# Message phase of a four-layer graph network on one core: TensorE takes the message products first in each turn

## What is computed

```python
et = edge_emb_W[edge_type]
m = relu(concat([x[src], et]) @ msg_W.T + msg_b)
agg = segment_sum(m, dst) / clip(deg, 1)
h = x + agg @ upd_W.T + upd_b
x1 = (h - mean(h)) * rsqrt(var(h) + 1e-5) * ln_g + ln_b
x  = layernorm(x + x1)
```

## Time and profile before

| | before |
|---|---|
| median of 3 runs | 2558.56 us (2558.45 to 2558.84) |
| profiled execution, its own time | 2568.89 us |
| its span | 2567.1 us |
| busy: TensorE | 1396.4 us (54%) |
| busy: VectorE | 1565.7 us (61%) |
| busy: ScalarE | 861.6 us (34%) |
| busy: GpSimd | 1825.5 us (71%) |
| mean granted clock of TensorE | 0.761 |

### The profile page before, as it was taken

One profiled execution on the slowest core, in us unless ns is written; L12 is line 12 of the kernel. 1 busy time (PEld: TensorE's weight loads), 2 busy tenths in 40 slices (PEclk: granted clock), 3 DMA queues, 4 the chain that ended last, 5 costly groups with the idle time before them and its releaser, 6 DMA issues. The chain is left out here.

```text
span 2567.1 us, 21864 instructions
## 1 busy us (share of the span) xinstructions
PE 1396.4 (54%) x4580; PEld 726.2 (28%) x4580; DVE 1565.7 (61%) x4901; ACT 861.6 (34%) x1813; POOL 1825.5 (71%) x1444
## 2 busy tenths in 40 slices
PE   6788488887455456619698376445454650011111
PEld 1344244444222222303343144222222330011110
DVE  8889377778537776967989544233344555434433
ACT  0111166776425455754687322011012320000000
POOL 5764677787188888617666388788775878778887
PEclk8899699999677777859899688677777875555555
DMA  1111244443244554625565476577796873323331
GB/s 24 26 34 37 78 114 134 123 125 91 75 101 98 127 127 111 149 63 126 123 148 141 84 215 194 135 200 173 173 170 195 224 200 93 85 63 72 75 71 43
DMA packets 358129, 297.95 MB, mean 116 GB/s; under 512 B 110941, under 2 KB 312428, under 8 KB 357981
## 3 DMA queue, kind: packets, MB, share of 16 engines
q1 hardware_dynamic: 260397, 225.43, 32.5%
q0 software_dynamic: 97600, 71.11, 14.5%
HBM read 199.75 MB, written 96.70 MB: 115 GB/s over the span
## 5 line engine op out<-in xcount | busy, mean ns | idle before, releaser
L2201 DVE TENSOR_TENSOR_SCAN tl_S<-tl_same,tl_S,tl_pX 128x500 f32<-128x500 bf16 x96 | 120.3, 1253 | 324.4 <-issue 172.6
L2090 PE MATMUL tl_pX<-k_ident,tl_ga 125*128 125x125 f32 x400 | 84.1, 348 | 428.3 <-DMA tl_ga<-table_TE,k_s_idxE 328.2
L480 POOL DMA_INDIRECT tl_ga<-table_TE,k_s_idxE x200 | 244.2, 1221 | 63.4 <-issue 58.8
L2090 PEld LDWEIGHTS tl_pX<-k_ident,tl_ga 125*128 125x128 f32 x400 | 57.5, 177 | 443.8 <-DMA tl_ga<-table_TE,k_s_idxE 338.7
L480 POOL DMA_INDIRECT eq_ga<-table_T,k_idxS x100 | 128.0, 1280 | 65.5 <-ACT eq_y L1794 37.3
L480 POOL DMA_INDIRECT at_ga<-x,k_src x100 | 139.5, 1395 | 43.4 <-issue 25.2
L480 POOL DMA_INDIRECT ms_ga<-table_T,k_idxS x100 | 143.3, 1433 | 36.4 <-issue 30.2
L480 POOL DMA_INDIRECT tl_ga<-table_TH,k_send x100 | 122.6, 1226 | 56.3 <-issue 55.7
L1270 PE MATMUL tl_pCon<-dr_BC,dn_cT 128*128 128x512 f32 x196 | 130.5, 754 | 54.0 <-ACT dn_cT L1277 27.3
L282 POOL DMA_INDIRECT table_ptab<-k_ef,ix_scatI x100 | 124.2, 1242 | 48.8 <-issue 48.8
L480 POOL DMA_INDIRECT at_gb<-xw,at_dstI x100 | 129.8, 1298 | 30.5 <-issue 30.5
(11 more groups left out here) (465 smaller groups left out, 4406.2 us busy)
## 6 DMA issues: line engine op xcount, KB each, us to landing
dr_x<-x SPq DMA_DIRECT2D x97, 256.0 KB
result<-dr_o SPq DMA_DIRECT2D x97, 256.0 KB
dm_xT<-xT SPq DMA_DIRECT2D x32, 768.0 KB
tl_fac<-table_dinv SPq DMA_DIRECT2D x50, 250.0 KB
table_T<-at_y SPq DMA_DIRECT2D x50, 224.0 KB
table_T<-ms_y SPq DMA_DIRECT2D x50, 224.0 KB
table_T<-eq_y SPq DMA_DIRECT2D x50, 224.0 KB
table_TE<-tl_y SPq DMA_DIRECT2D x50, 224.0 KB
```

The costliest lines, as they stand in the source:

```text
L480: nc.gpsimd.indirect_dma_start(out=buf[:, k, :], out_offset=None, in_=table, in_offset=bass.IndirectOffsetOnAxis(ap=index[:, CT * c + k:CT ...
L2090: last = nc.tensor.transpose(pX[j % 2][:, k * TP:(k + 1) * TP], ga[j % RG][:, k, :], K["ident"][0:TP, 0:TP])
L2201: nc.vector.tensor_tensor_scan(S[i][:], same[j % RM][:], pX[i][:, 0:CE], 0.0 if j % NC == 0 else S[1 - i][:, CE - 1:CE], ALU.mult, ALU.add ...
```

## The change

In TensorE's loop of the message phase, the step `message(s + 1)` moves from behind `turn(s + 2)` to the head of the turn. The order becomes message products, row transposes, transposes of gathered rows, update, moments. The steps themselves, their waits and their semaphores, and all other engines, stay as they are.

```diff
             for s in range(-2, NC + 1):
+                if live(s + 1):
+                    message(s + 1)
                 if live(s - 1):
                     rows(s - 1)
                 if live(s + 2):
                     turn(s + 2)
-                if live(s + 1):
-                    message(s + 1)
                 if live(s):
                     update(s)
                     dn.moments(pe, MA + s)
```

## The result

| | before | after |
|---|---|---|
| median of the runs (11 each) | 2558.84 us | 2565.99 us |
| ratio, 95% interval | | 1.0026 [1.0015, 1.0038] |
| profiled span | 2567.1 us | 2565.5 us |
| busy: TensorE | 1396.4 us | 1421.5 us |
| busy: VectorE | 1565.7 us | 1581.2 us |

The kernel became slower by 0.26%, 6.7 us by the ratio (7.2 by the medians); 5.4 us were forecast. The span of the profiled execution is 1.6 us shorter than before's, against the median. What follows therefore reads stretches, and says under e7 and e8 where the 1.6 us come from. VectorE's 15.5 us more of busy time are not the order's: a second profile of after (e8) has 1567.4 us.

What follows compares the result with a forecast made beforehand. GpSimd's DMA issues, then VectorE's queue after about 1003 us, were taken to bound the message phase. 0.54 + 0.70 + 2.1 + 2.1 = 5.4 us on 2558.56 gave 2564.0 us, range 2558.2 to 2568.5 us.

Steps and rivals of the forecast that it cites:

- What bounds the phase: Message phase: GpSimd's DMA issues set the pace to about 1003 us, then VectorE's queue, ten turns in 120.4 us.
- rival C: GpSimd's gathers: fewer long instructions, gather 9 us earlier, 2555 us, chance 0.08; mirror, +9 us and more, 0.06.
- the last gather-bound transposes: Sign in TensorE's turn 16: again near 1003 us; over 2 us off 1003.17 would mean GpSimd's pace depends on the order.
- Earlier message products gain nothing: ScalarE's relu of the message products stays behind its own `source` and `norm1`; value 0.
- The products' own time: Turns after s = 16 and 20: 1.68 us of products delay transposes; less slack, 0.54 + 0.70 us late.
- The clock under moments: TensorE at s = 16 and 20: `moments` starts at half clock after an idle gap, +2.1 us each.
- Rival A: TensorE's clock rises despite the gap in one or both turns: +3.3 or +1.24 us, 2559.8 to 2561.9 us; chance 0.22.
- Where the wait shows: VectorE's `gained` after turns 16 and 20 would wait about 2.6 and 2.8 us for `norm1`, where before had none.
- Rival B: Late transposes in turn 17 stay hidden by VectorE's slack: 2558.6 us, at most half a us from before; chance 0.12.
- From the profile to the medians: Whole kernel: profiled execution 2568.89 to 2574.3 us; its 10.3 us above the median carried over, giving 2564.0 us.
- the question of 0.2%: Whole kernel against the 5.1 us bound: slower by over 0.2% chance 0.45, within 0.49, faster 0.06.

Runs made afterwards that it cites:

- e7: The unchanged kernel before, profiled once more for scatter; 121.8 us from `gained(14)` to `gained(24)`, against 120.4 us in its first profile.
- e8: The changed kernel after, profiled once more for scatter; 126.3 us from `gained(14)` to `gained(24)`, as in its first profile.
- e4: Against after: eight products of the identity, never read, added behind `update` in turns with s % 4 = 0; median 2566.62 us, ratio 0.9999 to before.
- e2: Against after: message products back behind the transposes of gathered rows in turns with s % 4 = 0 only; median 2570.34 us, ratio 1.0012 to before.
- e1: Against after: VectorE's `keep_moments` moved ahead of `residual`, so `moments` needn't wait for it; median 2568.49 us, ratio 1.0011 to before.
- e9: Against before: VectorE's `keep_moments` moved ahead of `residual`, TensorE's order as in before; ratio 0.9996 to before, 119.7 us from `gained(14)` to `gained(24)`.

## Why the prediction held

*What bounds the phase.* Right. The end of the phase is the last gather awaited plus VectorE's queue. The part of GpSimd scatters by several us and took no side; rival C, faster or slower through GpSimd, has nothing for it. One of the prediction's own signs did show against it: the last gather-bound transposes came at 1000.67, more than 2 us off 1003.17. The sign was too tight, for in e7 the unchanged kernel came 2.4 us off.

*Earlier message products gain nothing.* Right: in after ScalarE's relu of turn 16 starts right behind its `norm1` as before, and no step of VectorE from `gained(14)` on became shorter.

*The products' own time, 0.54 + 0.70 us.* Right in mechanism and size: with the clock up, e4 shows 0.57 and 0.85, e2 0.57 in the one turn with a fast start.

*The clock under moments, 2.1 us twice.* Right in mechanism; the first was 1.97 us, the second 2.7. In the three profiles of after the first lies between 1.5 and 2.0 us and the second between 2.5 and 2.7, so 2.1 was near the first and too small for the second. That the step had to be priced from one stretch of another burst, and came out this near, is partly luck. In turn 20 the way there differs too: the clock was up over the transposes and fell in a wait for `ms_mean` that the products used to fill. The sum with the measured values is 1.68 + 1.97 - 1.14 = 2.5 and 1.68 + 2.7 - 0.98 = 3.4 us; the steps grew by 2.54 and 3.36. What failed is the silent assumption that before always has the clock up at this point. In e7 it had not, in both turns; so the difference of the two orders is 4.5 to 6 us, not one number. Rival A, that the clock is up when `moments` starts in after, came in none of the 15 late `moments` of its three profiled executions.

*Where the wait shows.* Partly wrong. I expected 2.6 and 2.8 us ahead of `gained`. VectorE reaches `residual` first, which waits for the row transposes, so 1.29 and 2.14 us appear there and only 1.09 and 1.08 us ahead of `gained`. The sum is 5.6 us, against 5.4.

*Rival B (hidden anyway)* holds only where `moments` isn't late: e1 and e9.

*From the profile to the medians.* The forecast for the profiled execution, 2574.3 us, missed: it took 2567.38, less than before's 2568.89. A profiled execution is a single run, runs scatter by several us, and the 10.3 us by which before's lay above its median were no property of the kernel; in after it is 1.4 us. The forecast of the median didn't suffer, since it adds the 5.4 us to a median.

The ratios (0.26%, or 6.7 us, in the first comparison, 0.22% on the chip of e9) agree with the stretch within their intervals, and can't tell 4.5 from 6 us. Nor do they decide the question of 0.2% to which the prediction gave its chances: the interval of the first comparison runs from 0.15 to 0.38%.

## What to carry to other kernels

Ask of a step that is moved to the head of a turn what it now stands in front of in the one turn in four where the queue runs through without a pause; its slack there, not its average, is the price. Ask too what work it leaves behind: a burst cut in two around a wait may cost more by the clock (2.0 and 2.7 us here) than the moved step by its place (1.7 us). And a slow clock on an engine off the path is free until another engine awaits the work done under it.

## What the runs showed of the hardware

The length of an idle gap alone didn't tell whether the granted clock fell in it. In all four cases TensorE had worked 4.9 to 6.5 us before the gap, from the row transposes or the transposes of gathered rows to the end of `update`. The clock stayed up through 3.09 us in turn 20 of before, and was down after 2.79 us in turn 20 of e2, 2.00 us in turn 16 of e7 and 2.61 us in its turn 20. So the same place in the same kernel runs at either level from one profiled execution to another, and 1.4 us of the phase follow it (120.4 against 121.8). The page "TensorE: Matmul & The Clock Gate" of the Trainium skill, section "Part 1: The HAM clock gate (the "warmup" mystery)", says that the moment at which the clock rises under sustained matmuls varies from run to run, with when the first of them falls. The gaps above show such a variation for the fall.
